# Two phases joined without the first one's last waits, and two weight rows loaded into other buffers

## What is computed

```python
def xattn(x, kv, wq, wk, wv, wo):             # 1 head of 512
    k = concatenate([kv, x @ wk.T], axis=1)
    v = concatenate([kv, x @ wv.T], axis=1)
    attn = softmax((x @ wq.T) @ k.T / sqrt(512))
    return (attn @ v) @ wo.T

def attn(x, W_Q, b_Q, W_K, b_K, W_V, b_V, W_O, b_O):   # 16 heads of 128
    Q, K, V = x @ W_Q + b_Q, x @ W_K + b_K, x @ W_V + b_V
    Q, K = rope(Q), rope(K)
    return softmax(causal(Q @ K.T / sqrt(128))) @ V @ W_O + b_O

x = x + xattn(layernorm(x), ctx, ...)         # called x1 in the kernel
x = x + attn(layernorm(x), ...)
x = x + ffn(layernorm(x), ...)
```

## Time and profile before

| | |
|---|---|
| median of 3 runs | 1384.15 us (1381.96 to 1385.51) |
| the profiled execution, its time | 1385.5 us |
| its span, first to last instruction | 1383.7 us |
| granted PE clock, mean over the span | 0.988 of full |
| PE busy | 1340.2 us (97%) |
| DVE busy | 1005.3 us (73%) |
| ACT busy | 508.6 us (37%) |
| POOL busy | 380.9 us (28%) |
| 16 DMA engines, one hardware queue | 25.2% of their time |

### The profile page before, as it was taken

The page is one execution under the profiler, slowest core; times in us unless marked ns, Lnnn a source line. Parts: engine busy times, 40 slices in busy tenths (PEclk is TensorE's granted clock), DMA queues, the critical chain, the costliest instruction groups (busy, mean ns, idle before and its releaser), DMA issues. The chain is left out here.

```text
span 1383.7 us, 23386 instructions
## 1 busy us (share of the span) xinstructions
PE 1340.2 (97%) x9216; PEld 777.6 (56%) x9216; DVE 1005.3 (73%) x2285; ACT 508.6 (37%) x1252; POOL 380.9 (28%) x302
## 2 busy tenths in 40 slices
PE   8999999967999999999999999999899999999998
PEld 6666666634666666666666666654344434434443
DVE  6444444257888888898888887856999698688684
ACT  3222222232343433433343433330001386666671
POOL 0000000002222222222222122211133296748571
PEclk9999999989999999999999999999999999999999
DMA  8555544613110022011101021077761000000001
GB/s 336 206 199 198 202 187 183 228 65 122 32 32 25 23 63 62 31 32 59 49 32 31 32 62 32 19 197 215 189 213 61 1 1 1 0 1 31 1 31 61
DMA packets 36902, 122.56 MB, mean 89 GB/s; under 512 B 4281, under 2 KB 4921, under 8 KB 28089
## 3 DMA queue, kind: packets, MB, share of 16 engines
q1 hardware_dynamic: 36520, 118.19, 25.2%
q10 hardware_dynamic: 272, 2.88, 0.8%
HBM read 95.89 MB, written 25.17 MB: 87 GB/s over the span
## 5 line engine op out<-in xcount | busy, mean ns | idle before, releaser
L871 POOL TENSOR_TENSOR hd_rotated<-hd_products 64x512 f32<-64x512 f32 x32 | 40.3, 1259 | 742.5 <-DVE hd_products L1122 742.5
L191 PE MATMUL psum<-hd_xt_hi,hqk_hi 128*128 128x512 f16 x512 | 194.6, 380 | 1.6 <-DVE hd_xt_lo L1096 1.6
L192 PE MATMUL psum<-hd_xt_lo,hqk_hi 128*128 128x512 f16 x512 | 194.3, 379 | 0.0
L193 PE MATMUL psum<-hd_xt_hi,hqk_lo 128*128 128x512 f16 x512 | 194.3, 379 | 0.0
L1508 POOL TENSOR_TENSOR ff_part<-ff_part 128x512 f32<-128x512 f32 x88 | 129.9, 1479 | 83.1 <-DVE ff_part L1640 82.9
L1640 DVE SCALAR_TENSOR_TENSOR ff_part<-psum,gu_scale,ff_part 128x512 f32<-128x512 f32 x176 | 123.0, 742 | 36.4 <-PE psum L1534 30.7
L191 PE MATMUL psum<-hd_wv_hi,hd_xt_hi 128*128 128x256 f16 x512 | 140.3, 274 | 4.5 <-DVE hd_wv_lo L1101 4.5
L192 PE MATMUL psum<-hd_wv_lo,hd_xt_hi 128*128 128x256 f16 x512 | 140.4, 274 | 0.0
L193 PE MATMUL psum<-hd_wv_hi,hd_xt_lo 128*128 128x256 f16 x512 | 140.4, 274 | 0.0
L1533 PE MATMUL psum<-ff_xt_hi,gu 128*128 128x512 f16 x352 | 134.4, 382 | 5.4 <-DVE ff_part L1640 4.8
L1534 PE MATMUL psum<-ff_xt_lo,gu 128*128 128x512 f16 x352 | 134.2, 381 | 0.0
(11 more groups left out here) (188 smaller groups left out, 3004.4 us busy)
## 6 DMA issues: line engine op xcount, KB each, us to landing
xa_kv_t<-in_ctx_t_dram SPq DMA_DIRECT2D x16, 1024.0 KB, 5.4
xa_kv<-in_ctx_dram SPq DMA_DIRECT2D x16, 1024.0 KB, 4.9
w_rows<-in_head_weights_dram SPq DMA_DIRECT2D x12, 1024.0 KB, 7.8
z_scratch<-hd_z_hi SPq DMA_DIRECT2D x32, 256.0 KB, 2.6
z_scratch<-hd_z_lo SPq DMA_DIRECT2D x32, 256.0 KB, 3.3
w_rows<-z_scratch SPq DMA_DIRECT2D x8, 1024.0 KB, 8.6
hqk_lo<-z_scratch SPq DMA_DIRECT2D x8, 1024.0 KB, 7.1
xn<-in_x_dram SPq DMA_DIRECT2D x8, 512.0 KB, 4.0
```

Of the source, the lines that this page charges most:

```text
L191: pe.matmul(out, lh, rh, start=(first and i == 0), stop=False)
L192: pe.matmul(out, lh, rl, start=False, stop=False)
L193: last = pe.matmul(out, ll, rh, start=False, stop=(final and i == k - 1))
```

## The change

Cross attention's stream on SP no longer waits for the stores of x1 and for the rows of weights. The semaphores `rows_loaded` and `x1_stored` are now made outside of both phases and handed to both. In `heads_phase`:

- SP, ACT and DVE each wait for all x1 stores before their first work that writes an `hd_` buffer (`wait_x1_stored`). PE and POOL don't.
- V's row 3 is loaded into `rotated`, V's row 2 into `xn`; rows 0 and 1 stay in `w_rows`. Row 3 is the first DMA of the phase, ahead of the six tables; row 2 follows them, and waits until PE has transposed `xn`.
- ACT waits for rows 0 and 1 by the semaphores of the phase before, and for rows 2 and 3 by one of each.
- DVE clears `pt_hi` and `pt_lo` first, ahead of `xt_lo`.
- POOL waits for all of `wv_lo` before it writes `rotated` for the first time, and SP before it loads the next tile into `xn`.

```diff
@@ xattn_phase
-        rows_loaded = [sem("rows0_loaded"), sem("rows1_loaded")]
...
-        x1_stored = [sem("even_x1_stored"), sem("odd_x1_stored")]
...
             sp.wait_ge(head_lo_done, NH)
             load_head_rows(NH + 1)
-            for n in range(2):
-                sp.wait_ge(x1_stored[n], 32 * (NH // 2))
-            for i in range(2):
-                sp.wait_ge(rows_loaded[i], 16 * (2 + (NH + 2) // 2))
@@ heads_phase
-        loaded = [sem("rows0_loaded"), sem("rows1_loaded")]
+        wo_loaded, late_rows_loaded = sem("wo_loaded"), {k: sem(f"rows{k}_loaded") for k in range(2, KD)}
...
+        def wait_x1_stored(eng):
+            for n in range(2):
+                eng.wait_ge(x1_stored[n], 32 * (NH // 2))
+
+        wv_rows = [w_rows[:, 0, :], w_rows[:, 1, :], xn[:, :, :].rearrange("p b d -> p (b d)"),
+                   rotated[:, :, :, :].rearrange("p a b t -> p (a b t)")]
...
         @block.sync
         def _(sp):
+            def load_rows(k):
+                sp.dma_start(wv_rows[k], head_weights[(2 * KD + k) * P:(2 * KD + k + 1) * P, :]).then_inc(late_rows_loaded[k], 16)
+
+            wait_x1_stored(sp)
+            load_rows(3)
             for dst, src in ((cos, rope_cos), (sin, rope_sin), (mask, causal)):
...
             sp.dma_start(bias_v[:, :], b_v).then_inc(small_loaded_z_stored, 16)
-            for k in range(2, KD):
-                sp.wait_ge(w_lo_done, k - 1)
-                sp.dma_start(w_rows[:, k % 2, :], head_weights[(2 * KD + k) * P:(2 * KD + k + 1) * P, :]).then_inc(loaded[k % 2], 16)
+            for k in range(KD):
+                banks.wait_filled(sp, {}, ("x", k))
+            load_rows(2)
...
                     sp.wait_ge(xt_hi_done, s.t * KD + KD)
+                    sp.wait_ge(w_lo_done, KD)
                     sp.dma_start(xn[:, :, :], rows_of(s.t * TILE + TILE)).then_inc(x_loaded, 16)
...
@@ POOL's step
+                if not s.att:
+                    pool.wait_ge(w_lo_done, KD)
                 banks.wait_moved(pool, s.runs_proj, ("q", 1))
@@ ACT
+            wait_x1_stored(act)
             first_halves({})
             for k in range(KD):
-                if k >= 2:
-                    act.wait_ge(loaded[k % 2], 16)
-                act.activation(wv_hi[:, k, :], w_rows[:, k % 2, :], ACT.Copy, scale=WS).then_inc(w_hi_done, 1)
+                if k < 2:
+                    act.wait_ge(first_rows_loaded[k], 16 * (2 + (NH + 2) // 2))
+                else:
+                    act.wait_ge(late_rows_loaded[k], 16)
+                act.activation(wv_hi[:, k, :], wv_rows[k], ACT.Copy, scale=WS).then_inc(w_hi_done, 1)
@@ DVE
+            wait_x1_stored(dve)
+            dve.memset(pt_hi[:, :, :, :], 0.0)
+            dve.memset(pt_lo[:, :, :, :], 0.0).then_inc(zeros_set, 1)
             second_halves({}, 0)
             for k in range(KD):
                 dve.wait_ge(w_hi_done, k + 1)
-                dve.scalar_tensor_tensor(wv_lo[:, k, :], w_rows[:, k % 2, :], WS, wv_hi[:, k, :],
+                dve.scalar_tensor_tensor(wv_lo[:, k, :], wv_rows[k], WS, wv_hi[:, k, :],
                                          ALU.mult, ALU.subtract).then_inc(w_lo_done, 1)
...
             dve.wait_ge(bias_scaled, 2)
-
-            dve.memset(pt_hi[:, :, :, :], 0.0)
-            dve.memset(pt_lo[:, :, :, :], 0.0).then_inc(zeros_set, 1)
```

More of the change, by code:

```diff
@@ L207, in xattn_phase @@
 def xattn_phase(nc, psum, ident, x_rows, ctx_kv, ctx_t, wq, wk, wv, wo, identity, x1_rows, w_hi, w_lo, w_rows, xn, stat,
-                head_weights, hqk_hi, hqk_lo):
+                head_weights, hqk_hi, hqk_lo, rows_loaded, x1_stored):
     with ExitStack() as ctx:
@@ L773, in heads_phase @@
                 rope_cos, rope_sin, causal, w_o, wo_hi, wo_lo, z_scratch, first_z, small_loaded_z_stored,
-                early, early_sems, b_o, shifts, gu_scales, gu_codes):
+                early, early_sems, b_o, shifts, gu_scales, gu_codes, first_rows_loaded, x1_stored):
     with ExitStack() as ctx:
@@ L906, in load_wo @@
                 sp.wait_ge(w_lo_done, KD + 2 * t)
-                sp.dma_start(w_rows[:, 0, :], w_o[:, t * (4 * D):(t + 1) * (4 * D)]).then_inc(loaded[0], 16)
+                sp.dma_start(w_rows[:, 0, :], w_o[:, t * (4 * D):(t + 1) * (4 * D)]).then_inc(wo_loaded, 16)
             def step(s):
@@ L1081, in step @@
                 if s.pair == 3:
-                    act.wait_ge(loaded[0], s.t * 16 + 32)
+                    act.wait_ge(wo_loaded, s.t * 16 + 16)
                     act.activation(wo_hi[:, s.t * 4:s.t * 4 + 4, :].rearrange("p n m -> p (n m)"), w_rows[:, 0, :], ACT.Copy,
@@ L1743, in whole_kernel @@
         early, early_sems = Early(hqk_hi, hqk_lo), EarlySems(nc, ctx)
+        rows_loaded = [ctx.enter_context(nc.semaphore(f"rows{i}_loaded")) for i in range(2)]
+        x1_stored = [ctx.enter_context(nc.semaphore(f"{n}_x1_stored")) for n in ("even", "odd")]
         xattn_phase(nc, psum, ident, x.rearrange("b s d -> (b s) d"), ctx_2048, ctx_t, wq, wk, wv, wo,
-                    identity, x1, wo_hi, wo_lo, w_rows, xn, stat, head_weights, hqk_hi, hqk_lo)
+                    identity, x1, wo_hi, wo_lo, w_rows, xn, stat, head_weights, hqk_hi, hqk_lo,
+                    rows_loaded, x1_stored)
         heads_phase(nc, psum, ident, x1, xn, stat, head_weights, hqk_hi, hqk_lo, w_rows, b_q, b_k, b_v,
                     rope_cos, rope_sin, causal, w_o, wo_hi, wo_lo, z, first_z, z_stored,
-                    early, early_sems, b_o, shifts, gu_scales, gu_codes)
+                    early, early_sems, b_o, shifts, gu_scales, gu_codes, rows_loaded, x1_stored)
         gu, gu_scale = sb("gu", [P, KD, GU], F16), sb("gu_scale", [P, 2 * FB * KD], F32)
```

## The result

| | before | changed |
|---|---|---|
| median of 20 runs | 1385.67 us | 1375.91 us |
| span of the profiled execution | 1383.7 us | 1371.7 us |

The ratio is 0.9935, with a 95% interval of 0.9922 to 0.9948: 9.0 us less, between 7.2 and 10.8 (the two medians themselves lie 9.8 us apart). The median of the kernel before is 1.5 us above the one that the forecast started from, since 17 more runs were made of it.

The account below looks back on a forecast made before the run. PE is 97% busy; its idle time at the join, where first scores wait for DVE's `rotated` behind V's row loads, sets the end. Multiplications at 315.0 instead of 324.14: 9.1 us off median 1384.15 gives 1375.0; range 1372.0 to 1379.5.

Parts of the forecast that it names:

- The waits at the end of cross attention: Join of the phases: SP leaves at 297.7, heads phase begins at 298.2 instead of 302.6; ACT's new wait costs nothing.
- PE isn't late: q and k projections end at 313.8, or 315.5 with a half-clock stretch; DVE needs the first bank at 315.
- Rows 2 and 3: SP's load queue: row 2 issued 302.15, landing 308.2 after row 1, row 3 and 0.7 us of tables in turn.
- the sign that I had set myself: Profile after the change: the forecast is wrong if, among other signs, row 2 lands after 309.
- My bounds for the landing: Row 2's load: 306.95 with free queues (4.8 us), 308.2 with everything ahead in turn; 308.2 taken.
- rival A: Row 2 comes late, its load taking 8.0 or 9.8 us: 7.2 or 5.4 off, 1377.0 or 1378.8; chance 0.14.
- The ceiling of 10.4 us: Join: the earliest landing, 306.95, gives 10.4 us off; DVE's own chain of four (304.4 to 313.4) allows no more.
- The 358 GB/s of the Trainium skill: A core's HBM share: 1 MB takes 2.9 us, so row 2 lands at 308.7, 0.5 us later than by the rows.
- Weights and memsets: ACT and DVE in the join: multiplications start 6.8 us behind row 2's landing, at 315.0; memsets leave the chain.
- B: Rival at the join: the new phase's code must be fetched, nearest price 2.0 us; at most 1377.0; chance 0.06.
- C: Rival in the heads phase: new half-clock stretches, 1.7 us each, give the gain back: 1380 to 1384; chance 0.08.
- D: Rival, slower: row 2 held up in the queue; gain gone at landing 317.3, 0.3% slower from 321.5; chance 0.04.

Follow-up runs that it names:

- the second execution: The changed kernel, unedited, run once more beside the one with rows 2 and 3 in `products`, on the same chip: 1377.54 us, ratio 0.9941.

## Why the prediction was right, and where it was off

The time (1375.0 forecast, 1375.91 measured) came out as forecast, and so did the way there, but for the landing of row 2. The steps can be compared one by one:

| distance from the last x1 addition, us | forecast | measured |
|---|---|---|
| PE's transposes begin | 2.0 | 1.96 |
| row 3 goes out | 2.8 | 2.86 |
| q and k projections begin | 7.1 | 6.6 |
| row 2 goes out | 6.0 | 6.70 |
| row 2 has landed (ACT begins) | 12.0 | 13.39 |
| from there to the first multiplication | 6.8 | 6.65 |
| first scores | 28.9 | 30.21 |
| gained in the join | 9.15 | 7.83 |

*The waits at the end of cross attention.* Right: 0.45 us pass from SP's last issue (293.75 + 0.43) to PE's first transpose (294.63), where 0.5 was read before. The waits for the x1 stores on ACT and DVE cost nothing that counts: ACT waited for the store until 295.52, but later 4.35 us for row 2.

*PE isn't late.* Right, and with the half-clock stretch that I had allowed for: the 48 matmuls of q and k took 11.9 us instead of 10.5. The table by stages of the changed kernel:

```profile
294.60:297.50 2.90, 2.86 (x16) 2.48 (x16) 1.76 (x4) 1.68 (x3) 0.00 (x0) 0.65 0.96 321
...
299.30:311.20 11.90, 11.90 (x48) 4.94 (x48) 7.69 (x4) 6.13 (x4) 0.00 (x0) 0.87 0.45 167
311.20:312.50 1.30, 0.09 (x1) 0.00 (x0) 1.30 (x2) 0.00 (x0) 0.00 (x0) 1.00 0.00 0
312.50:317.90 5.40, 5.34 (x48) 4.62 (x48) 5.37 (x11) 0.60 (x1) 2.26 (x2) 1.00 0.78 272
```

They were done at 311.2, 1.3 us ahead of the last `wv_lo`, and V's projection, at full clock this time, 5 us ahead of the scores.

*Rows 2 and 3.* This is the term that was mis-sized, by 1.35 us. I let a megabyte pass in 2.7 us and the tables in 0.7, 11.0 us from the issue of row 1 to the landing of row 2; it was 12.3 (293.75 to 306.06), and that holds the whole 1.35. The issues of the changed kernel (size, us from issue to landing) show where:

```profile
w_rows<-in_head_weights_dram SPq DMA_DIRECT2D x1, 1024.0 KB, 5.2
hd_rotated<-in_head_weights_dram SPq DMA_DIRECT2D x1, 1024.0 KB, 6.9
xn<-in_head_weights_dram SPq DMA_DIRECT2D x1, 1024.0 KB, 6.7
hd_cos<-in_rope_cos_dram SPq DMA_DIRECT2D x1, 32.0 KB, 6.1
```

Row 1 took 5.2 us, where I had 4.9. Row 3 (issued at 295.53) landed 3.5 us behind row 1, where I had 2.7. Row 2 landed 3.6 behind row 3, where I had 3.4. So most of the error stands ahead of row 3, not between it and row 2, and the first table, issued behind row 3 (295.91), landed at 302.0 and row 3 at 302.4: the loads didn't pass in turn, as my sum had let them. With the tables issued behind all three rows the distance from row 1's issue to the last landing was 11.1 us (295.24 to 306.36), and 10.85 and 11.5 with the rows in `products` (293.14 to 303.99, 293.30 to 304.77), where my sum had 10.3 without the tables. With the tables between them it was 12.3, 12.8 (late memsets) and 13.3 (the changed kernel again). The means are 1.6 us apart, where I had 0.7 for the tables.

The issue was late as well: I took the six tables to occupy SP for 2.7 us, as before; they took 3.3 (295.91 to 298.48 + 0.73), because the last two, issued while two loads of 1 MB were under way, took 0.62 and 0.73 us instead of 0.43. No run shows that this by itself moved the landing: in the second execution row 2 went out a little earlier (6.55 for 6.70) and landed a microsecond later.

By the sign that I had set myself, a landing after 309, which is 12.8 behind the addition, this step was wrong: it was 13.4 and 14.35. ACT stood 4.35 us for row 2 where I had named some 2, since it was also done with rows 0 and 1 0.9 earlier than forecast (9.0 behind the addition). My bounds for the landing (306.95 to 308.2, so 4.8 to 6.05 us for 6.7 and 7.8) were too narrow above, and rival A, the late row, held a real part of the truth in a mild form.

*The ceiling of 10.4 us* that I read from DVE's own chain was wrong too, though the sum didn't rest on it. In the changed kernel DVE began its first `wv_lo` 7.3 us behind the addition, where I had 8.2, and in the run with the rows in `products` 6.7; there the join gained 38.04 - 26.56 = 11.5 us.

*The 358 GB/s of the Trainium skill* (DMA: Bandwidth & Descriptors, Bandwidth). That section gives it as what each core gets when both cores of a pair stream; here one core ran, and the runs don't show it as a limit: with both rows in `products` ACT's starts on them lie 303.99 - 301.41 = 2.58 us apart, 1.05 MB at 406 GB/s. Its sum, 308.7, would have come nearer to what was measured, but its step of 2.9 us for a megabyte is neither these 2.6 nor the 3.5 between rows 1 and 3.

*Weights and memsets.* Right: 6.65 us from the landing to the multiplications, and the run with late memsets puts them at 0.95 us.

*The rivals.* B, a fetch of instructions: the only queue at work between 293 and 300 was again SP's, with 350 packets, and PE began within half a microsecond of SP's last issue. (That the branches here lead to code not held, as the prediction took them to, no run shows; they cost no visible fetch.) C, a gain given back: the time from the scores to the end fell by 0.7 us; over all profiled executions it lies between 1046.0 and 1051.3 us with no relation to the edit that I can see, a spread as large as most of the differences here. D: row 2 landed 13.4 us behind the addition, 7.8 before the point at which the gain would have been gone (317.3 - 296.16 = 21.1).

That the whole time agrees to 0.1 us in the gain (9.0 for 9.15) is luck within the interval. What the profiles show for the join is 7.8 us, and 6.9 in the second execution; the rest of the 9.0 is smaller than what the interval leaves open, and I can't attribute it.

## What to carry to other kernels

Ahead of a barrier between two phases, ask of each wait who needs what it waits for: here PE needed neither the stores nor the weights, and moving each wait to its user was worth 5.7 us alone. Two edits that both bring a load forward needn't add up (5.7 and 4.9 gave 6.4 here), since the load then meets other loads on its way and other waits ahead of its issue. The last load that the chain needs should go out first, ahead of small transfers that nobody waits for yet, and into a buffer whose first writer comes late (`products` here), so that it needs no wait of its own. And to compare two executions, measure from an event just before the edit: the spans differed by 12.0 us, of which 3.5 were the clock at the start.

## What the runs showed of the hardware that I hadn't expected

- Issuing a DMA on SP isn't of fixed length: 0.43 us for a table while at most one load of 1 MB was under way (the two runs that undo half of the change), 0.48 to 0.74 for the fifth and sixth where two were ahead of them, and 0.43 to 0.74 where all six stood behind three.
- The same load in the same program, behind the same two, landed 6.7 us after its issue in one execution and 7.8 in another; with no more than one load of 1 MB and some tables ahead of it 4.8 to 5.15.
- A small transfer behind a large one need not land behind it: the cos table of 32 KB, issued 0.38 us after row 3 on the same queue, landed 0.4 us before it. Yet it took 6.1 us, where in the kernel before, with nothing else under way, it took 1.6.
- PE's clock was halved within its transposes (0.65 over 2.9 us) although the pause ahead of them had shrunk from 6.5 to 2.0 us, and stayed so into the projections. With the same pause of 2.0 us one execution with the rows in `products` kept the full clock through the transposes and was halved in the projections instead. So the shorter pause can shift the stretch at half clock, but in none of the ten executions did it take it away. That execution's stages, the first with transposes (294.0 to 296.0), the second with projections (from 298.6):

```profile
295.00:297.00 2.00, 0.95 (x9) 0.71 (x7) 1.92 (x4) 2.00 (x5) 0.00 (x0) 1.00 0.99 356
...
299.00:301.00 2.00, 2.00 (x7) 0.75 (x5) 2.00 (x2) 1.52 (x1) 0.00 (x0) 0.50 1.04 406
```
